# Attention outputs for two heads at a time, the own keys' products on 32-row tiles

## The chip, the cores and the metric

The kernel runs on one core of a Trainium2 chip. The metric is the device time of one execution in microseconds (us), the median of several runs. The whole model fragment is one program; the changed part is its attention stage.

## The reference, cut to what matters

Four layers are applied to a state of 64 sequences of 32 tokens and 512 features, each added to the state. The first three are a dense layer that is picked by sequence and two low-rank layers. The fourth is attention with a paged cache. Of it the change touches the line that starts `o =`:

```python
valid = jnp.concatenate([valid_c, jnp.ones((bsz, seqlen), dtype=bool)], axis=1)
k_all = jnp.concatenate([kc, k], axis=1)      # 512 cached keys, then the 32 own keys
v_all = jnp.concatenate([vc, v], axis=1)
k_all = jnp.repeat(k_all, rep, axis=2)        # 8 key heads, each for 4 query heads
v_all = jnp.repeat(v_all, rep, axis=2)
scores = jnp.einsum('bqhd,bkhd->bhqk', q, k_all) * SCALE
scores = jnp.where(valid[:, None, None, :], scores, -1e+30)
probs = jax.nn.softmax(scores, axis=-1)
o = jnp.einsum('bhqk,bkhd->bqhd', probs, v_all)
```

## The kernel before, in words

The program goes through the layers one after the other; attention takes from about 887 us to about 2106 us of the profiled execution.

**Units.** Attention works on units. A unit is one sequence and one key head: 4 query heads x 32 tokens are its 128 query rows, against 544 keys (512 cached and 32 own). There are 64 sequences x 8 key heads (HK) = 512 units. The main loop runs over pairs of sequences, that is 16 units (UNITS), numbered j = 0 to 15 in the pair; u is the unit's number in the whole run. I call the part of the loop body for one j a step, and count steps by j modulo 8.

**A step of TensorE (PE).** For each j it issues, in this order:
1. `scores` of unit u + 2: six matmuls of 128 x 272, three for each half of the keys, since both operands are split into a high and a low part (L102, L103, L104). They go to `ps_s`, half j % 2.
2. `outputs` of unit u - 4 (OG = 4): four fp32 matmuls of 128 x 128 against the cached values (L1672), and one against the own values (L1675). The trace shows every fp32 matmul as two weight loads (LDWEIGHTS) and two MATMUL records.
3. `transpose` of unit u: four 128 x 128 transposes of its probabilities into `ps_pt` (L1649). In steps 3 and 7 a transpose of the own keys' probabilities of the last four units follows (L1655), and in step 7 one of the sums of the probabilities (L1657).

**The own keys.** The own keys' probabilities of four units are put side by side (`p_own`, 4 x 32 columns), and transposed in one piece, so the 128 rows of `pto_sb` hold the 32 keys of unit 0, then those of unit 1, and so on. The own values `vo_sb` lie on the same 32 rows for each unit and are zero on the other 96, so before the change a product over all 128 rows gives the 32 keys' share. That transpose is written to a spare corner of `ps_s` (function `spare`), which is in the bank that the scores of the odd unit u + 2 also use. For that reason `transpose` waits ahead of L1655 until VectorE has read these scores:

```python
if j % OG == OG - 1:
    if not (last and j == UNITS - 1):
        pe.wait_ge(masked, u + 3)
    pe.wait_ge(gathered, u + 1)
    mm = pe.transpose(spare(1, P), p_own[:, g % 2, :, :].rearrange("p u k -> p (u k)"), ident[:, :])
```

`masked` counts the units whose scores VectorE has turned into masked, scaled scores with their maximum, so u + 3 means that unit u + 2 is done.

**VectorE (DVE)** in a step: in steps 0 and 4 the copy of the transposed own probabilities (`copy_own`, L1588), in step 0 also the reciprocal of the sums (L1595); then it waits for the scores of u + 2, gathers the own probabilities of u + 1 (L1580, waits for ScalarE's exponential of that unit), masks u + 2 (L1390), makes the low part of one piece of the next keys or queries (L1365; pieces stand in steps 0, 1, 2, 3, 4 and 7, the one in step 1 a short one, none in 5 and 6), copies the outputs of four units (`copy_o`, L1603, in steps 1 and 5), and in step 2 makes a mask (L1384).

**ScalarE (ACT)** in a step: the exponential of u + 2 (L1370), the high part of a piece (L1359), the copy of the transposed probabilities of u (L1548). **GpSimd (POOL)** issues the loads of queries, own keys and own values (L1484), the indirect loads of cached values (L1490) and the store of the outputs (L1496). SyncE (SP) issues the loads of key pages.

Semaphores set the order between the engines; each engine goes through its own list strictly in order. `pv_done` counts units whose outputs are finished, `o_ready` counts copies of outputs, `pt_ready` and `pto_ready` the copies of transposed probabilities.

Of the kernel before, what the change touches and what calls it, by code (L numbers as in the profile page):

```python
# [25 lines left out]
P = 128  # L26
NSEQ, SEQ, D = 64, 32, 512
# [6 lines left out]
DH, HQ, HK = 128, 32, 8  # L34
REP = HQ // HK
NPAGE, PSIZE, NPP = 64, 32, 16
NKEY = NPP * PSIZE
# [69 lines left out]
def later(t, n):  # L107

    return not isinstance(t, int) or t >= n
# [1133 lines left out]
UNITS = 2 * HK  # L1243
OG = 4
# [27 lines left out]
def attention(nc, m, place, both, pool_sems, k_pages, v_pages, table, lens, key_at, q_t, k_own, v_own, o_t, inv_t):  # L1272
# [37 lines left out]
    pv_done = m.sem("pv_done")  # L1310
# [10 lines left out]
    def group_before(i, j, n):  # L1321

        g = j // OG - n
        return (i, g) if g >= 0 else (i - 1, g + UNITS // OG)

    def spare(half, rows):

        return ps_s[0:rows, 1, half, D - P:D]
# [133 lines left out]
    def gpsimd(pool):  # L1462
# [29 lines left out]
                    bass.IndirectOffsetOnAxis(ap=rows_now[:, p, c:c + 1], axis=0)).then_inc(v_loaded[p], 16)  # L1492

        def store(s, p):
            pool.wait_ge(o_ready, (HK // OG) * (s + 1))
            pool.dma_start(o_t[bass.ds(s, 1)], o_sb[:, p, :, :].rearrange("p h q -> p (h q)"))\  # L1496
                .then_inc(o_stored[p], 16)
            pool.wait_ge(inv_ready, s + 1)
            pool.dma_start(inv_t[bass.ds(s, 1)].rearrange("s (h q) -> (s h) q", h=HK), inv_sb[:, p, :])\
                .then_inc(inv_stored[p], 16)  # L1500
# [67 lines left out]
    def vector(dve):  # L1568
# [25 lines left out]
                dve.wait_ge(inv_stored[p], 16 * i)  # L1594
            dve.reciprocal(inv_sb[:, p, :], spare(0, HK)).then_inc(inv_ready, 1)  # L1595

        def copy_o(i, g):

            p = g // 2
            dve.wait_ge(pv_done, UNITS * i + OG * (g + 1))  # L1600
            if later(i, 1):
                dve.wait_ge(o_stored[p], 16 * i)
            dve.tensor_copy(o_sb[:, p, (g % 2) * OG:(g % 2 + 1) * OG, :], ps_o[:, g % 2, :, :])\  # L1603
               .then_inc(o_ready, 1)

        dve.wait_ge(s_done, 2)
        gather(0, 0)
# [2 lines left out]
        def pair(i, last):  # L1610
            for j in range(UNITS):
                u, s, p = UNITS * i + j, 2 * i + j // HK, j // HK
                if j % OG == 0 and later(u, OG):
                    copy_own(*group_before(i, j, 1))
                    if j % HK == 0:
                        invert(*group_before(i, j, 1)[:1], (1 - p))
                if not (last and j >= UNITS - 2):
                    wait_for_scores(2 * i + (j + 2) // HK, u + 2, (j + 2) % UNITS)
                if not (last and j >= UNITS - 1):
                    gather(u + 1, (j + 1) % UNITS)  # L1620
                if not (last and j >= UNITS - 2):
                    mask_and_max(dve, u + 2, (j + 2) % UNITS)
                if not later(u, HK - 1):
                    for c in FIRST_LO[j]:
                        lo_part(dve, 1, 1, c)
                elif not (last and j >= HK - 1):
                    ahead = 2 if j % HK == HK - 1 else 1
                    for c in LO_AT[j % HK]:
                        lo_part(dve, s + ahead, (p + ahead) % 2, c)
                if j % OG == 1 and later(u, 2 * OG):  # L1630
                    copy_o(*group_before(i, j, 2))
                if j % HK == 2 and not (last and p):
                    make_mask(dve, s + 1, 1 - p)
            if last:
                copy_own(i, UNITS // OG - 1)
                invert(i, 1)
                copy_o(i, UNITS // OG - 2)
                copy_o(i, UNITS // OG - 1)

        in_pairs(dve, NSEQ // 2, pair)  # L1640

    def tensor(pe):
# [14 lines left out]
                mm = pe.transpose(spare(0, HK), total[:, p, :], ident[:, :])  # L1657
            mm.then_inc(t_done, 1)

        def outputs(i, u, j):  # L1660
            p, h, g = j // HK, j % HK, j // OG
            if h == 0:
                pe.wait_ge(v_loaded[p], 16 * (NPP // PPP) * (i + 1))
                pe.wait_ge(own_v_loaded[p], 16 * OG * (i + 1))
            if j % OG == 0 and later(u, 2 * OG):
                pe.wait_ge(o_ready, (UNITS // OG) * i + g - 1)
            pe.wait_ge(pt_ready, u + 1)
            if not later(u, 1):
                pe.wait_ge(both.out_ready, ALL_STEPS)
            out = ps_o[:, g % 2, j % OG, :]  # L1670
            for c in range(NKEY // P):
                pe.matmul(out, v_sb[p][:, c, h * DH:(h + 1) * DH], pt_sb[:, j % OG, c, :],  # L1672
                          start=(c == 0), stop=False)
            pe.wait_ge(pto_ready, UNITS // OG * i + g + 1)
            pe.matmul(out, vo_sb[p][:, g % 2, j % OG, :], pto_sb[:, g % 2, :],  # L1675
                      start=False, stop=True).then_inc(pv_done, 1)

        pe.wait_ge(both.normed_ready, ALL_STEPS)

        def pair(i, last):  # L1680
            for j in range(UNITS):
                u = UNITS * i + j
                if not (last and j >= UNITS - 2):
                    scores(pe, i + (j + 2) // UNITS, u + 2, (j + 2) % UNITS)
                if j >= OG:
                    outputs(i, u - OG, j - OG)
                elif later(u, OG):
                    outputs(i - 1, u - OG, UNITS - OG + j)
                transpose(u, j, last)
            if last:  # L1690
                for j in range(UNITS - OG, UNITS):
                    outputs(i, UNITS * i + j, j)

        in_pairs(pe, NSEQ // 2, pair)

# [303 lines left out]
```

## Time and profile before

| | |
|---|---|
| median of 3 runs | 2503.28 us (2501.54 to 2503.5) |
| the profiled execution, its own time | 2503.97 us |
| its span in the trace | 2502.3 us |
| PE busy / weight loads / DVE / ACT / POOL, share of the span | 96% / 88% / 71% / 64% / 24% |
| stretch of attention in the steady loop | 918.9 to 2100.6 us |

The span is the time from the first to the last instruction in the trace; the other 1.7 us of that execution lie around it. Busy shares are means over all stages; attention is nearly half of the time and is read by itself below.

### The profile page before, as it was taken

To read this page: it belongs to the slowest core of one execution; us is meant where nothing else is said; L and a number is where in the kernel's file an instruction comes from. 1 tells how busy PE (TensorE), PEld (TensorE's weight loads), DVE (VectorE), ACT (ScalarE), POOL (GpSimd) and SP (SyncE) were. 2 spreads that over 40 slices of the span, in tenths; PEclk is the share of its full clock that TensorE was granted. 3 is DMA by queue.
4 is the path that set the end of the run, shared out by engine and by line. 5 is a ranking of instruction groups with operands and counts; after the bars stand their busy time and mean duration, and the time that the engine had idled before them with its cause. 6 is when DMAs were issued, how large, how long until landed. Compare 5 with 4: busy or idle time off the path is not lost. (4 is left out here: it accounts for less than half of the span.)

```text
span 2502.3 us, 54645 instructions
## 1 busy us (share of the span) xinstructions
PE 2406.1 (96%) x16070; PEld 2192.6 (88%) x16071; DVE 1780.0 (71%) x3632; ACT 1603.3 (64%) x3311; POOL 599.2 (24%) x896
## 2 busy tenths in 40 slices
PE   6899899999999979999999999999999996799999
PEld 4688788888888879999999999999999996588887
DVE  5454329999898968878878878878878875544443
ACT  3233337777787778888888888888888884311111
POOL 1200040000000044444444444444444441000000
PEclk9899999999999979999999999999999998899999
DMA  6622333333334388888888888888888874766664
GB/s 221 185 81 64 117 122 90 101 102 97 100 114 124 94 289 300 289 288 303 291 289 300 289 290 301 293 288 302 291 287 294 300 255 156 281 210 221 208 209 145
DMA packets 373752, 536.83 MB, mean 215 GB/s; under 512 B 49314, under 2 KB 263010, under 8 KB 369826
## 3 DMA queue, kind: packets, MB, share of 16 engines
q1 hardware_dynamic: 301538, 311.62, 38.8%
q0 software_dynamic: 70016, 221.30, 25.8%
q10 hardware_dynamic: 2112, 2.89, 0.4%
q8 instruction: 38, 0.62, 0.1%
q14 instruction: 48, 0.39, 0.1%
HBM read 437.35 MB, written 98.30 MB: 214 GB/s over the span
## 5 line engine op out<-in xcount | busy, mean ns | idle before, releaser
L1672 PE MATMUL both_ps_o<-att_pt,att_v 128*128 128x128 f32 x4096 | 540.1, 275 | 0.0
L1370 ACT ACTIVATE att_prob<-att_prob,att_shift 128x544 f32<-128x544 f32 x512 | 384.4, 751 | 206.5 <-DVE att_shift L1390 197.0
L1672 PEld LDWEIGHTS both_ps_o<-att_pt,att_v 128*128 128x128 f32 x4096 | 504.8, 191 | 0.0
L1390 DVE CUSTOM_DVE_ANT_0 att_prob<-both_ps_s,att_mask 128x544 f32<-128x544 f32 x512 | 364.5, 712 | 0.0
L102 PE MATMUL both_ps_s<-att_k_hi,att_q_hi 128*128 128x272 f32 x1024 | 339.5, 332 | 4.6 <-DVE att_k_lo L1365 4.6
L1365 DVE TENSOR_TENSOR att_k_lo<-att_k_raw,att_k_hi 128x1024 fp32r<-128x1024 f32 (+1 forms) x320 | 338.5, 1058 | 1.9 <-ACT att_k_hi L1359 1.9
L1649 PE MATMUL both_ps_pt<-both_ident,att_prob 128*128 128x128 f32 x2048 | 309.4, 274 | 6.8 <-ACT att_prob L1370 5.2
L104 PE MATMUL both_ps_s<-att_k_hi,att_q_lo 128*128 128x272 f32 x1024 | 298.3, 291 | 0.0
L1548 ACT ACTIVATE att_pt<-both_ps_pt 128x512 f32<-128x512 f32 x512 | 294.6, 575 | 2.3 <-PE both_ps_s L1657 1.2
L103 PE MATMUL both_ps_s<-att_k_lo,att_q_hi 128*128 128x272 f32 x1024 | 295.4, 289 | 0.0
L1359 ACT ACTIVATE att_k_hi<-att_k_raw 128x1024 fp32r<-128x1024 f32 (+1 forms) x320 | 292.7, 915 | 0.0
L1484 POOL DMA_DIRECT2D att_vo<-v_own x256 | 139.9, 547 | 557.5 <-PE both_ps_o L1675 496.6
L1490 POOL DMA_INDIRECT att_v<-in_v_pages,att_rows_now x256 | 251.1, 981 | 86.0 <-issue 86.0
L1580 DVE TENSOR_REDUCE att_p_own<-att_prob 128x32 f32<-128x32 f32 x512 | 90.8, 177 | 237.0 <-PE both_ps_s L104 224.2
L1649 PEld LDWEIGHTS both_ps_pt<-both_ident,att_prob 128*128 128x128 f32 x2048 | 242.8, 142 | 7.5 <-ACT att_prob L1370 5.5
L1826 ACT ACTIVATE out_o_hi<-out_o 128x2048 fp32r<-128x2048 f32 x32 | 61.4, 1918 | 289.1 <-DVE out_o L1853 282.0
L102 PE MATMUL out_ps_y<-out_w_hi,out_o_hi 128*128 128x512 f32 x512 | 203.0, 397 | 36.2 <-DVE out_w_lo L1846 32.4
L103 PE MATMUL out_ps_y<-out_w_lo,out_o_hi 128*128 128x512 f32 x512 | 202.2, 395 | 0.0
L104 PE MATMUL out_ps_y<-out_w_hi,out_o_lo 128*128 128x512 f32 x512 | 202.0, 395 | 0.0
L102 PEld LDWEIGHTS both_ps_s<-att_k_hi,att_q_hi 128*128 128x128 f32 x1024 | 195.0, 190 | 6.8 <-DVE att_k_lo L1365 5.1
L1675 PE MATMUL both_ps_o<-att_pto,att_vo 128*128 128x128 f32 x1024 | 198.2, 275 | 0.0
L103 PEld LDWEIGHTS both_ps_s<-att_k_lo,att_q_hi 128*128 128x128 f32 x1024 | 196.2, 192 | 0.0
(209 smaller groups left out, 5025.7 us busy)
## 6 DMA issues: line engine op xcount, KB each, us to landing
att_k_raw<-in_k_pages SPq DMA_DIRECT2D x1024, 128.0 KB, 4.8
q_t<-qkv_out_t SPq DMA_DIRECT2D x128, 256.0 KB, 2.3
att_q_raw<-q_t POOLq DMA_DIRECT2D x64, 512.0 KB, 7.4
o_t<-att_o POOLq DMA_DIRECT2D x64, 512.0 KB, 6.9
out_o<-o_t SPq DMA_DIRECT2D x32, 1024.0 KB, 6.1
out_inv<-inv_t SPq DMA_DIRECT2D x32, 1024.0 KB, 6.6
both_w_stage<-in_w_qkv SPq DMA_DIRECT2D x12, 1024.0 KB, 5.2
l_w_stage<-in_w SPq DMA_DIRECT2D x8, 1024.0 KB, 7.1
```

What stands on the lines that cost most here:

```text
L102: pe.matmul(out, xh, wh, start=start, stop=False)
L103: pe.matmul(out, xh, wl, start=False, stop=False)
L104: return pe.matmul(out, xl, wh, start=False, stop=stop)
L1359: act.activation(hi, raw, ACT.Copy).then_inc(hi_done, 1)
L1365: dve.tensor_tensor(lo, raw, f32(hi), ALU.subtract).then_inc(lo_done, 1)
L1370: act.activation(prob[:, b, :], prob[:, b, :], ACT.Exp, bias=shift[:, b:b + 1], scale=-1.0, accum_out=total[:, j // HK, j % HK:j % HK + 1] ...
L1390: dve.tensor_tensor_reduce(out=prob[:, b, :].rearrange("p (a n) -> p a n", a=2), in0=ps_s[:, j % 2, :, 0:HALF], in1=mask[:, j // HK, :].re ...
L1490: pool.indirect_dma_start(v_sb[p][:, c, :], None, v_pages.rearrange("n k x -> (n k) x"), bass.IndirectOffsetOnAxis(ap=rows_now[:, p, c:c + ...
L1548: act.activation(pt_sb[:, j % OG, :, :], ps_pt[:, j % 2, :, :], ACT.Copy).then_inc(pt_ready, 1)
L1649: mm = pe.transpose(ps_pt[:, j % 2, c, :], prob[:, j % NB_P, c * P:(c + 1) * P], ident[:, :])
L1672: pe.matmul(out, v_sb[p][:, c, h * DH:(h + 1) * DH], pt_sb[:, j % OG, c, :], start=(c == 0), stop=False)
L1675: pe.matmul(out, vo_sb[p][:, g % 2, j % OG, :], pto_sb[:, g % 2, :], start=False, stop=True).then_inc(pv_done, 1)
```

## The change

The outputs are no longer made one unit a step. In every second step (j even) PE makes the outputs of two units, and in the others none. Each of the two units has a PSUM bank of its own (`ps_o[:, 0, 0, :]` and `ps_o[:, 1, 0, :]`). The eight products against cached values come first, then the two against own values; these now use the unit's own 32 rows of `vo_sb` and `pto_sb` alone, so that the two lie on different groups of 32 rows of the array. VectorE copies the two outputs together, 256 columns, at the end of the same step (before: 512 columns for four units, every fourth step). PE waits for that copy before the next two outputs. The store waits for four copies a sequence instead of two.

```diff
+    def units_before(i, j):
+
+        return (i, j - OG) if j >= OG else (i - 1, j - OG + UNITS)
...
-            pool.wait_ge(o_ready, (HK // OG) * (s + 1))
+            pool.wait_ge(o_ready, (HK // 2) * (s + 1))
...
-        def copy_o(i, g):
-
-            p = g // 2
-            dve.wait_ge(pv_done, UNITS * i + OG * (g + 1))
+        def copy_o(i, j):
+
+            p, h = j // HK, j % HK
+            dve.wait_ge(pv_done, UNITS * i + j + 2)
             if later(i, 1):
                 dve.wait_ge(o_stored[p], 16 * i)
-            dve.tensor_copy(o_sb[:, p, (g % 2) * OG:(g % 2 + 1) * OG, :], ps_o[:, g % 2, :, :])\
-               .then_inc(o_ready, 1)
+            dve.tensor_copy(o_sb[:, p, h:h + 2, :], ps_o[:, :, 0, :]).then_inc(o_ready, 1)
...
-                if j % OG == 1 and later(u, 2 * OG):
-                    copy_o(*group_before(i, j, 2))
+                if j % 2 == 0 and later(u, OG):
+                    copy_o(*units_before(i, j))
...
-        def outputs(i, u, j):
-            p, h, g = j // HK, j % HK, j // OG
-            if h == 0:
+        def outputs(i, j):
+
+            u, p, g = UNITS * i + j, j // HK, j // OG
+            if j % HK == 0:
                 pe.wait_ge(v_loaded[p], 16 * (NPP // PPP) * (i + 1))
                 pe.wait_ge(own_v_loaded[p], 16 * OG * (i + 1))
-            if j % OG == 0 and later(u, 2 * OG):
-                pe.wait_ge(o_ready, (UNITS // OG) * i + g - 1)
-            pe.wait_ge(pt_ready, u + 1)
+            if later(u, 2):
+                pe.wait_ge(o_ready, UNITS // 2 * i + j // 2)
             if not later(u, 1):
                 pe.wait_ge(both.out_ready, ALL_STEPS)
-            out = ps_o[:, g % 2, j % OG, :]
-            for c in range(NKEY // P):
-                pe.matmul(out, v_sb[p][:, c, h * DH:(h + 1) * DH], pt_sb[:, j % OG, c, :],
-                          start=(c == 0), stop=False)
+            for n in range(2):
+                h = (j + n) % HK
+                pe.wait_ge(pt_ready, u + n + 1)
+                for c in range(NKEY // P):
+                    pe.matmul(ps_o[:, n, 0, :], v_sb[p][:, c, h * DH:(h + 1) * DH], pt_sb[:, (j + n) % OG, c, :],
+                              start=(c == 0), stop=False)
             pe.wait_ge(pto_ready, UNITS // OG * i + g + 1)
-            pe.matmul(out, vo_sb[p][:, g % 2, j % OG, :], pto_sb[:, g % 2, :],
-                      start=False, stop=True).then_inc(pv_done, 1)
+            for n in range(2):
+                own = slice((j + n) % OG * SEQ, ((j + n) % OG + 1) * SEQ)
+                pe.matmul(ps_o[:, n, 0, :], vo_sb[p][own, g % 2, (j + n) % OG, :], pto_sb[own, g % 2, :],
+                          start=False, stop=True).then_inc(pv_done, 1)
...
-                if j >= OG:
-                    outputs(i, u - OG, j - OG)
-                elif later(u, OG):
-                    outputs(i - 1, u - OG, UNITS - OG + j)
+                if j % 2 == 0 and later(u, OG):
+                    outputs(*units_before(i, j))
                 transpose(u, j, last)
```

The order of instructions on PE, in a step 3 inside a sequence, with the step after it up to its first outputs. Names in brackets are the semaphores waited for; L1649, L1655, L1672 and L1675 of before are L1652, L1658, L1677 and L1682 after the change. Before:

```order
L104 MATMUL both_ps_s<-att_k_hi_4906,att_q_lo_4908 128x272
L1672 MATMUL both_ps_o<-att_pt,att_v_4910 128x128 [waits att_pt_ready]
L1672 MATMUL both_ps_o<-att_pt,att_v_4910 128x128 x3
L1675 MATMUL both_ps_o<-att_pto,att_vo_4911 128x128 [waits att_pto_ready]
L1649 MATMUL both_ps_pt<-both_ident,att_prob 128x128 [waits att_pt_ready,att_exp_done]
L1649 MATMUL both_ps_pt<-both_ident,att_prob 128x128 x3
L1655 MATMUL both_ps_s<-both_ident,att_p_own 128x128 [waits att_gathered,att_masked]
L102 MATMUL both_ps_s<-att_k_hi_4906,att_q_hi_4907 128x272 [waits att_masked]
```

After:

```order
L104 MATMUL both_ps_s<-att_k_hi_4906,att_q_lo_4908 128x272
L1652 MATMUL both_ps_pt<-both_ident,att_prob 128x128 [waits att_pt_ready,att_exp_done]
L1652 MATMUL both_ps_pt<-both_ident,att_prob 128x128 x3
L1658 MATMUL both_ps_s<-both_ident,att_p_own 128x128 [waits att_gathered,att_masked]
L102 MATMUL both_ps_s<-att_k_hi_4906,att_q_hi_4907 128x272 [waits att_masked]
```

Between the last scores matmul (L104) and the transpose of the own probabilities, which waits for `masked`, the five output matmuls are gone; they stand in the step before, with those of another unit.

On VectorE, at the end of a step 2 and the start of step 3 (L1365, L1384, L1580 and L1390 of before are L1369, L1388, L1584 and L1394 after). Before:

```order
L1365 TENSOR_TENSOR att_k_lo_4909<-att_k_raw_4904,att_k_hi_4906 128x4x8x32 [waits att_hi_done]
L1384 ISA
L1384 TENSOR_SCALAR att_mask<-att_key_at,att_lens_f 128x512
L1573 REGISTER_ALU
L1580 TENSOR_REDUCE att_p_own<-att_prob 128x32 [waits att_exp_done,att_t_done,att_s_done]
```

After:

```order
L1369 TENSOR_TENSOR att_k_lo_4903<-att_k_raw_4898,att_k_hi_4900 128x4x8x32 [waits att_hi_done]
L1607 COPY att_o<-both_ps_o 128x256 [waits pool_o_stored0,att_pv_done]
L1388 ISA
L1388 TENSOR_SCALAR att_mask<-att_key_at,att_lens_f 128x512
L1577 REGISTER_ALU
L1584 TENSOR_REDUCE att_p_own<-att_prob 128x32 [waits att_exp_done,att_t_done,att_s_done]
```

A copy of two units' outputs now stands in step 2, as in steps 0, 4 and 6, ahead of the gather and the masking of the next step.

## Rows read from the trace of the kernel before

**Rows 1.** The page's first part: busy time, share of the span, instructions.

```profile
PE 2406.1 (96%) x16070; PEld 2192.6 (88%) x16071; DVE 1780.0 (71%) x3632; ACT 1603.3 (64%) x3311; POOL 599.2 (24%) x896
```

**Rows 2.** Windows: busy us and instructions of each engine, clock, DMA share, GB/s.

```profile
1501.25:1520.02 18.77, 18.77 (x166) 18.75 (x164) 15.22 (x37) 15.62 (x31) 8.49 (x14) 1.00 0.85 293
918.90:2100.60 1181.70, 1181.70 (x10260) 1180.30 (x10259) 953.44 (x2256) 978.19 (x1881) 529.32 (x804) 1.00 0.86 287
```

**Rows 3.** Line L1657, once a sequence: duration in ns, first and last start.

```profile
L1657 PE MATMUL both_ps_s<-both_ident,att_total x64: 272/273/273, 919.0 to 2100.7; 128*8 128x128 f32 x64
```

**Rows 4.** Waits, 918.9 to 2100.6 us: us, times, longest. PE has none.

```profile
DVE att_p_own L1580 <- PE both_ps_s L104: 219.5, 285, 1.5
ACT att_prob L1370 <- DVE att_shift L1390: 192.2, 285, 1.3
POOL att_vo L1484 <- PE both_ps_o L1675: 496.6, 61, 14.5
```

**Rows 5.** Timeline of a step 3: start, duration (us), engine, line.

```profile
1508.88 0.29 PE L104 MATMUL both_ps_s<-att_k_hi,att_q_lo 128*128 128x272 f32 x1
1508.89 0.98 PEld L1672 LDWEIGHTS both_ps_o<-att_pt,att_v 128*128 128x128 f32 x8
...
1509.33 0.18 DVE L1580 TENSOR_REDUCE att_p_own<-att_prob 128x32 f32<-128x32 f32 x1
1509.43 0.71 DVE L1390 CUSTOM_DVE_ANT_0 att_prob<-both_ps_s,att_mask 128x544 f32<-128x544 f32 x1
...
1509.79 0.30 PEld L1675 LDWEIGHTS both_ps_o<-att_pto,att_vo 128*128 128x128 f32 x2
...
1510.01 0.47 PEld L1649 LDWEIGHTS both_ps_pt<-both_ident,att_prob 128*128 128x128 f32 x4
1510.07 0.08 DVE L1390 DVE_READ_ACCUMULATOR2_ANT att_shift<- 128x1 f32 x1
...
1510.19 0.75 ACT L1370 ACTIVATE att_prob<-att_prob,att_shift 128x544 f32<-128x544 f32 x1
1510.45 0.14 PEld L1655 LDWEIGHTS both_ps_s<-both_ident,att_p_own 128*128 128x128 f32 x1
...
1510.56 0.19 PEld L102 LDWEIGHTS both_ps_s<-att_k_hi,att_q_hi 128*128 128x128 f32 x1
...
1510.84 0.19 ACT L1370 ACTIVATION_READ_ACCUMULATOR att_prob<-att_prob,att_shift 128x1 f32 x1
...
1511.29 0.29 PE L104 MATMUL both_ps_s<-att_k_hi,att_q_lo 128*128 128x272 f32 x1
```

**Rows 6.** Timeline of the first step 3, where no outputs exist yet.

```profile
904.65 0.43 PE L104 MATMUL both_ps_s<-att_k_hi,att_q_lo 128*128 128x272 f32 x1
...
906.68 0.08 DVE L1390 DVE_READ_ACCUMULATOR2_ANT att_shift<- 128x1 f32 x1
...
906.81 0.18 PEld L1655 LDWEIGHTS both_ps_s<-both_ident,att_p_own 128*128 128x128 f32 x1 [1.26 <-DVE att_shift L1390]
```

**Rows 7.** Timeline around L1657, whose weights are 8 columns instead of 128.

```profile
1501.11 0.09 PEld L1657 LDWEIGHTS both_ps_s<-both_ident,att_total 128*8 128x8 f32 x1
1501.22 0.27 PE L1657 MATMUL both_ps_s<-both_ident,att_total 128*8 128x128 f32 x1
1501.22 0.19 PEld L102 LDWEIGHTS both_ps_s<-att_k_hi,att_q_hi 128*128 128x128 f32 x1
```

**Rows 8.** Groups by form, 1000 to 1800 us: busy us, mean ns.

```profile
L1675 PE MATMUL both_ps_o<-att_pto,att_vo 128*128 128x128 f32 x682 | 131.9, 275 | 0.0
L1603 DVE COPY att_o<-both_ps_o 128x512 f32<-128x512 f32 x85 | 58.2, 685 | 0.0
L1588 DVE COPY att_pto<-both_ps_s 128x128 f32<-128x128 f32 x85 | 24.1, 283 | 0.0
L1365 DVE TENSOR_TENSOR att_k_lo<-att_k_raw,att_k_hi 128x1024 fp32r<-128x1024 f32 x170 | 206.9, 1217 | 0.0
L1384 DVE TENSOR_SCALAR att_mask<-att_key_at,att_lens_f 128x512 f32<-128x512 f32 x43 | 20.6, 480 | 0.0
```

**Rows 9.** Windows at the start of attention; columns as in rows 2.

```profile
903.00:909.00 6.00, 5.14 (x24) 4.66 (x23) 5.22 (x15) 5.67 (x12) 5.30 (x8) 0.50 0.96 302
916.00:920.00 4.00, 4.00 (x37) 3.98 (x36) 2.57 (x8) 3.81 (x7) 0.00 (x0) 1.00 1.04 392
```

More of the change, by code:

```diff
@@ L1636, in pair @@
                 invert(i, 1)
-                copy_o(i, UNITS // OG - 2)
-                copy_o(i, UNITS // OG - 1)
+                for j in range(UNITS - OG, UNITS, 2):
+                    copy_o(i, j)
         in_pairs(dve, NSEQ // 2, pair)
@@ L1684, in pair @@
                     scores(pe, i + (j + 2) // UNITS, u + 2, (j + 2) % UNITS)
-                if j >= OG:
-                    outputs(i, u - OG, j - OG)
-                elif later(u, OG):
-                    outputs(i - 1, u - OG, UNITS - OG + j)
+                if j % 2 == 0 and later(u, OG):
+                    outputs(*units_before(i, j))
                 transpose(u, j, last)
             if last:
-                for j in range(UNITS - OG, UNITS):
-                    outputs(i, UNITS * i + j, j)
+                for j in range(UNITS - OG, UNITS, 2):
+                    outputs(i, j)
         in_pairs(pe, NSEQ // 2, pair)
```

## The prediction

> **What bounds the kernel now.** I read the page first: TensorE (PE) is busy for 96% of the span, everything else for 71% or less [rows 1]. A mean over stages proves little, so I read the attention loop by itself. One sequence takes 18.76 us: line L1657 runs once a sequence, 63 intervals between 919.0 and 2100.7 [rows 3]. In such a stretch PE is busy for all 18.77 us and its weight loads for 18.75, at full clock, while VectorE (DVE) works 15.22 and ScalarE (ACT) 15.62 [rows 2]. The waits agree: in the whole loop PE waits for nobody, while DVE waits 219.5 us for scores and ACT 192.2 us for DVE [rows 4]. So the loop goes at PE's pace; time taken from PE is gained and time in which PE stands is lost, one for one.
>
> The timeline of one step gives PE's parts, from one weight load to the next group's [rows 5]: the eight records against cached values 1508.89 to 1509.79, 0.90 us or 0.112 us a slot; the two of the own product 0.22; four transposes 1510.01 to 1510.45, 0.44; the own probabilities' transpose 0.11; the six score matmuls 1510.56 to 1511.29, 0.73. Without the extra transpose a step is 0.90 + 0.22 + 0.44 + 0.73 = 2.29 us.
>
> **What the change takes away.** The number of matmuls stays the same. A pair of units' own products takes 4 slots, 0.45 us. On 32 rows each still loads 128 columns and streams 128 columns, so alone it has no reason to be shorter; a gain comes only if the two units' products run beside each other on different rows. No row of the trace shows two row groups at work, so I bound it. No overlap: 4 slots, gain 0. Full overlap: 2 slots, 0.22 us a pair, 256 pairs, 57 us. Since each product is two records that must follow each other on the same rows, the second record of the first can overlap the first record of the second: 3 slots, 0.11 us a pair, 28 us. I take 3, in the middle between two ends for which no row speaks.
>
> In the Trainium skill, "TensorE: Matmul & The Clock Gate", Part 3, matmuls on different row groups run concurrently, and their weight loads overlap matmuls in flight; by it the pair would come near 2 slots and the gain near 57 us. No run here shows it yet.
>
> Changing between 128-row and 32-row tiles may cost something. The nearest row is L1657, whose weights are 8 columns wide instead of 128: its load starts at 1501.11, its matmul 0.11 us later, and the next full-width load at that same 1501.22 [rows 7]. Narrowing and widening cost nothing there, but in columns, not rows. Taken as it stands that row gives 0. The upper bound is that PE runs empty at each change: a record lasts 0.275 us [rows 8] against a slot of 0.11, so 0.165 us of tail, and 0.11 us more if the next weights can't load under it. Twice a pair, 256 pairs, is 84 to 141 us. I take 0 by the nearest row and keep the rest as a rival.
>
> The Trainium skill, "TensorEngine Tiling (Array Packing)", Key Properties, states that changing the tiling mode drains TensorE. By that rule the sum grows by those 84 to 141 us. The trace does not agree for the column case [rows 7].
>
> **What it moves, and the wait that this uncovers.** In steps 3 and 7, ahead of L1655, PE waits for `masked` of the unit whose scores it issued at the start of that same step. Let T be the start of the last score matmul, 1508.88. DVE gathers at T + 0.45 (1509.33), masks from 1509.43, and its accumulator read ends at 1510.15, T + 1.27 [rows 5]. PE gets to L1655's load at 1510.45, T + 1.57, because 0.90 + 0.22 of outputs and 0.44 of transposes stand between. So the wait has 0.30 us to spare. After the change steps 3 and 7 are odd steps: no outputs. PE gets there at T + 0.44 and stands until T + 1.27, plus some 0.05 for the release. In the first step 3, which has no outputs before the change either, exactly this wait is seen: the read ends at 906.76, the load starts at 906.81 after 1.26 us idle [rows 6]. Price: 1.27 + 0.05 - 0.44 = 0.88 us, in 128 groups less the first (already without outputs) and the last (doesn't wait), 126 x 0.88 = **111 us**. Behind L1655 on PE stand the next scores, for which DVE waits, so nothing makes it good.
>
> **Is DVE itself late there?** An odd step without L1655 is now 0.44 + 0.73 = 1.17 us, an even one 1.80 + 0.33 + 0.44 + 0.73 = 3.30. Step 2's gather needs the exponential of unit u + 1, which ACT makes from step 1's mask: that ends at T1 + 1.27, and ACT is done 0.88 us after such an end (1510.15 to 1511.03 [rows 5]). So the gather starts at T1 + 2.15, which is T2 + 0.98 instead of T2 + 0.45. Then DVE needs 0.82 for gather and mask, 1.22 for the low part, 0.42 for the copy and 0.48 for the mask of the next sequence [rows 8]: done at T2 + 3.92. T3 + 0.45 is T2 + 3.75. So in step 3 DVE is 0.17 us late, and PE's wait grows by as much once a sequence: 63 x 0.17 = 11 us. With 4 slots for the own products it is 0.06 (4 us), with 2 slots 0.28 (18 us). Step 7 follows a step with neither a low part nor a mask, and DVE is on time.
>
> **Edits at no cost.** A copy of 256 columns I put at 0.42 us: 0.283 for 128 and 0.685 for 512 [rows 8] give 0.134 for each further 128. Four a sequence instead of two are 1.67 against 1.37, so 0.30 us more for DVE, of 3.5 us that it is idle in 18.77 [rows 2]; outside step 2 idle time covers it. It costs PE only if it delays the next two outputs. These wait for the copy. In step 0 DVE is busy with copy, reciprocal, gather, mask, low part and ends the copy about T0 + 3.7; the next outputs come at T0 + 3.30 + 1.17 = T0 + 4.5: 0.8 us to spare. In steps 2, 4 and 6 there is more. GpSimd's loads of own values start when a sequence's outputs are done; it waits 496.6 us for that [rows 4], 8 us a sequence, and the outputs finish in step 2 instead of 3: hidden. The store of the outputs waits for a copy that now comes three steps earlier. The wait of PE for `pto_ready` moves behind eight more records, so it only gets easier.
>
> **The sum**, against the profiled execution's own 2503.97 us, which is 0.7 above the median of 2503.28: the wait +111, DVE's lateness +11, the own products -28, together +94: 2598 for such an execution, **2597 us** for the median. With 4 slots +111 + 4, 2618; with 2 slots +111 + 18 - 57, 2575.
>
> **Rivals.**
> - *The row tiles don't overlap* (the change doesn't do what it says): 2618. That a record's load already takes the whole slot of its matmul (weight loads 18.75 of 18.77 us [rows 2]) speaks for it: if loads go one by one, nothing is gained. It is one end of my forecast.
> - *The tile change empties PE.* 84 to 141 us on 2618, or on 2597 if the products overlap as well: 2681 to 2759. Against it: rows 7. For it: these are rows of the array, through which data flow, not columns.
> - *The clock falls.* At the start of attention, with PE standing now and again (busy 5.14 of 6.00 us), the granted clock was 0.50; with PE without gaps it was 1.00 [rows 9]. New gaps of about 0.9 to 1.2 us stand twice in some 20. Were a tenth of the loop's 1182 us of PE work done at 1.2 GHz instead of 2.4, that would add 118 us: about 2715. Against it: some 9 us of unbroken work between gaps.
> - *DVE becomes the bound.* If small gaps between its instructions grow with the new order by 0.5 us a sequence and reach PE, 32 us more: about 2629.
> - *Faster, on the other side:* the wait costs nothing since `masked` comes early. It decides from the point where stall and gain of a group of two pairs are equal: the release must come less than 0.44 + 0.22 = 0.66 us (3 slots) or 0.44 + 0.44 = 0.88 us (2 slots) after T, instead of 1.32. If it came within 0.44, the time would be 2503 - 28 = 2475, or 2446. Against it: the mask alone takes 0.71 us, and it can't start before the scores are done.
>
> **How the numbers follow.** My forecast, the wait of 0.88 us or a little more with own products in 2 to 4 slots, has a chance of 0.72: 2575 to 2618, with the small terms 2560 to 2635. The emptied PE gets 0.14, the clock 0.03, DVE as the bound 0.06, the faster case 0.05. The point is the likeliest's middle, 2597. The range reaches down to 2558 and up to 2670, which leaves out most of the emptied PE, the clock and the faster case, together 0.2. A measurement of this kernel tells about 0.2% (5 us) from no change. Faster by more: 0.05; within: 0.02; slower: 0.93.
>
> **What would show it.** Right: the waits list PE at the own probabilities' transpose (now L1658), released by DVE's shift, about 126 times, 0.9 us each, 110 to 130 us in all; a sequence takes about 20.3 us; the second of the own products' records start less than 0.11 us apart where row groups change. Wrong: no such wait, or a gap of 0.15 us or more between the last cached product, the own ones and the transposes (the tile change costs), or a clock under 1.00 in the loop. The forecast of the main term fails if DVE's reading of the scores ends much sooner than 1.27 us after T, or if PE comes later to L1658 than T + 0.44.

## The result and the profile after

The changed kernel takes 2635.4 us (median of 4 runs, 2633.8 to 2636.9), the kernel before 2503.4 (4 runs): a ratio of 1.0526, 95% interval 1.0508 to 1.0545, so 132 us slower. The profiled execution took 2635.22 us with a span of 2633.7.

The page's first part of the changed kernel, against [rows 1]:

```profile
PE 2471.8 (94%) x16070; PEld 2159.7 (82%) x16071; DVE 1804.0 (68%) x3760; ACT 1603.1 (61%) x3311; POOL 657.0 (25%) x896
```

TensorE (PE) issues the same 16070 matmuls, but its share fell. VectorE (DVE) has 128 more instructions, the additional copies. The windows, columns as in [rows 2], show the whole loop and one sequence:

```profile
920.40:2230.80 1310.40, 1249.18 (x10258) 1149.51 (x10259) 977.53 (x2382) 978.85 (x1881) 586.91 (x804) 1.00 0.77 258
1503.80:1524.60 20.80, 19.84 (x164) 18.36 (x165) 15.74 (x39) 15.74 (x31) 9.51 (x13) 1.00 0.81 273
```

The line that runs once a sequence and the two products, by tile (duration min/median/max in ns, first and last start), against [rows 3]:

```profile
L1660 PE MATMUL both_ps_s<-both_ident,att_total x64: 272/273/273, 920.5 to 2230.9; 128*8 128x128 f32 x64
L1682 PE MATMUL both_ps_o<-att_pto,att_vo x1024: 269/321/373, 911.0 to 2236.1; 32*128 32x128 f32 x171
L1607 DVE COPY att_o<-both_ps_o x256: 404/423/426, 911.5 to 2236.5; 128x256 f32<-128x256 f32 x128
```

A sequence takes (2230.9 - 920.5) / 63 = 20.80 us instead of 18.76. That is 2.04 us more, and 64 times 2.04 is 131 us: the whole loss is in this loop. Its granted clock is still 1.00, that is 2.4 GHz. The loop has 1310.4 us, and PE is busy for 1249.2 of them where it had been busy without a gap; but the busy time itself also grew by 67 us with as many matmuls, so the listed gaps needn't be all of it. Busy time rests on modelled ends of matmuls; below I go by the starts of weight loads.

The waits from 920 to 2200 us, nearly the whole loop (us, times, longest), against [rows 4] where PE had none:

```profile
POOL att_vo L1488 <- PE both_ps_o L1682: 560.1, 60, 15.3
ACT att_prob L1374 <- DVE att_shift L1394: 249.2, 369, 1.0
DVE att_p_own L1584 <- PE both_ps_s L104: 146.9, 184, 0.9
DVE att_p_own L1584 <- ACT att_prob L1374: 102.0, 123, 1.0
PEld both_ps_s L1658 <- DVE att_shift L1394: 88.5, 123, 0.7
DVE att_o L1607 <- PE both_ps_o L1682: 61.1, 122, 0.8
PE both_ps_s L1658 <- DVE att_shift L1394: 59.4, 123, 0.5
PEld both_ps_s L102 <- issue: 9.2, 29, 0.3
```

The forecast wait is there: at the transpose of the own probabilities (now L1658), released by DVE's shift, 123 times in 61.5 sequences, that is in every group. PE's weight loads stand 0.72 us each time. DVE also waits 61.1 us for the products at its new copies; no wait of PE for these copies is listed, so that costs nothing. The last line is new: 29 times 0.3 us of "issue" ahead of scores, which nobody releases.

The timeline of an even step and of the following step 3 of the changed kernel, against [rows 5] (start, duration, engine, line; in brackets the idle time before and its releaser):

```profile
1504.64 1.88 PEld L1677 LDWEIGHTS both_ps_o<-att_pt,att_v 128*128 128x128 f32 x16
1506.64 0.30 PEld L1682 LDWEIGHTS both_ps_o<-att_pto,att_vo 32*128 32x128 f32 x4
1506.65 0.49 PE L1682 MATMUL both_ps_o<-att_pto,att_vo 32*128 32x128 f32 x4
1507.06 0.42 PEld L1652 LDWEIGHTS both_ps_pt<-both_ident,att_prob 128*128 128x128 f32 x4
1507.45 0.19 PEld L102 LDWEIGHTS both_ps_s<-att_k_hi,att_q_hi 128*128 128x128 f32 x1
...
1512.68 0.48 DVE L1388 TENSOR_SCALAR att_mask<-att_key_at,att_lens_f 128x512 f32<-128x512 f32 x1
1512.93 0.29 PE L104 MATMUL both_ps_s<-att_k_hi,att_q_lo 128*128 128x272 f32 x1
1512.94 0.48 PEld L1652 LDWEIGHTS both_ps_pt<-both_ident,att_prob 128*128 128x128 f32 x4
1513.26 0.19 DVE L1584 TENSOR_REDUCE att_p_own<-att_prob 128x32 f32<-128x32 f32 x1
1513.36 0.72 DVE L1394 CUSTOM_DVE_ANT_0 att_prob<-both_ps_s,att_mask 128x544 f32<-128x544 f32 x1
1514.00 0.08 DVE L1394 DVE_READ_ACCUMULATOR2_ANT att_shift<- 128x1 f32 x1
1514.14 0.14 PEld L1658 LDWEIGHTS both_ps_s<-both_ident,att_p_own 128*128 128x128 f32 x1 [0.72 <-DVE att_shift L1394]
1514.22 0.19 PEld L102 LDWEIGHTS both_ps_s<-att_k_hi,att_q_hi 128*128 128x128 f32 x1
```

Two things are to be seen. In the even step, 16 slots of cached values should take 1.81 us by [rows 5], and the first load on 32 rows should come at 1506.45; it comes at 1506.64, 0.19 us late. The four products on 32 rows then last 0.42 us until the transposes' load at 1507.06, though they overlap: a narrower window of the same timeline has the second pair of their loads only 0.11 us behind the first.

```profile
1506.75 0.19 PEld L1682 LDWEIGHTS both_ps_o<-att_pto,att_vo 32*128 32x128 f32 x2
```

In the step without outputs the own transpose stands from about 1513.38 until 1514.14, 0.06 us after DVE's read of its accumulator ends (1514.08).

To account for a sequence I averaged, over some 60 of them, the time from the first weight load of each group of matmuls to that of the next. V: cached values, W: own products, T: transposes up to the next group, P: own probabilities' transpose, Q: transpose of the sums, S: scores.

```
per pair of units (us)      V      W      T       per sequence: T+P step 3   T+P step 7   Q      all
before                    1.808  0.444  0.439                   0.548        0.548        0.109  18.78
after                     1.998  0.420  0.388                   1.274        1.254        0.255  20.84
```

So of about 2.06 us a sequence: the change of row tile costs 0.19 us ahead of the own products, leaves these at 0.42 instead of the 0.22 that two slots take, and gives 0.05 back in the transposes: 0.115 a pair net or 0.46 a sequence (30 us in all). The wait is 0.726 + 0.706 = 1.43 (92 us). Q's stretch is 0.15 longer, which is the "issue" of the table above (9 us).

### The profile page after: what moved, and what is told of

The parts are those of the page before. It is cut to its first block and busy times, and to the rows that moved or that the text cites. A ratio compares the mean times of both kernels' runs of the same rounds, so it can differ in the third digit from the quotient of the medians.

```text
span 2633.7 us, 55206 instructions
## 1 busy us (share of the span) xinstructions
PE 2471.8 (94%) x16070; PEld 2159.7 (82%) x16071; DVE 1804.0 (68%) x3760; ACT 1603.1 (61%) x3311; POOL 657.0 (25%) x896
## 5 line engine op out<-in xcount | busy, mean ns | idle before, releaser
L1677 PE MATMUL both_ps_o<-att_pt,att_v 128*128 128x128 f32 x4096 | 499.5, 275 | 0.6 <-DVE att_o L1607 0.6
L1677 PEld LDWEIGHTS both_ps_o<-att_pt,att_v 128*128 128x128 f32 x4096 | 481.9, 192 | 0.8 <-DVE att_o L1607 0.7
L1394 DVE CUSTOM_DVE_ANT_0 att_prob<-both_ps_s,att_mask 128x544 f32<-128x544 f32 x512 | 364.6, 712 | 0.0
L1369 DVE TENSOR_TENSOR att_k_lo<-att_k_raw,att_k_hi 128x1024 fp32r<-128x1024 f32 (+1 forms) x320 | 338.8, 1059 | 4.3 <-ACT att_k_hi L1363 1.9
L1652 PE MATMUL both_ps_pt<-both_ident,att_prob 128*128 128x128 f32 x2048 | 322.8, 280 | 6.6 <-ACT att_prob L1374 5.0
L1494 POOL DMA_INDIRECT att_v<-in_v_pages,att_rows_now x256 | 306.0, 1195 | 81.2 <-issue 81.2
L104 PE MATMUL both_ps_s<-att_k_hi,att_q_lo 128*128 128x272 f32 x1024 | 297.4, 290 | 0.0
L1584 DVE TENSOR_REDUCE att_p_own<-att_prob 128x32 f32<-128x32 f32 x512 | 90.1, 176 | 275.1 <-PE both_ps_s L104 155.2
L1652 PEld LDWEIGHTS both_ps_pt<-both_ident,att_prob 128*128 128x128 f32 x2048 | 229.8, 141 | 38.1 <-ACT att_prob L1374 5.3
L104 PE MATMUL out_ps_y<-out_w_hi,out_o_lo 128*128 128x512 f32 x512 | 201.6, 394 | 0.0
L104 PEld LDWEIGHTS both_ps_s<-att_k_hi,att_q_lo 128*128 128x128 f32 x1024 | 194.3, 190 | 0.0
```

What stands on the lines that cost most here:

```text
L104: return pe.matmul(out, xl, wh, start=False, stop=stop)
L1369: dve.tensor_tensor(lo, raw, f32(hi), ALU.subtract).then_inc(lo_done, 1)
L1394: dve.tensor_tensor_reduce(out=prob[:, b, :].rearrange("p (a n) -> p a n", a=2), in0=ps_s[:, j % 2, :, 0:HALF], in1=mask[:, j // HK, :].re ...
L1494: pool.indirect_dma_start(v_sb[p][:, c, :], None, v_pages.rearrange("n k x -> (n k) x"), bass.IndirectOffsetOnAxis(ap=rows_now[:, p, c:c + ...
L1652: mm = pe.transpose(ps_pt[:, j % 2, c, :], prob[:, j % NB_P, c * P:(c + 1) * P], ident[:, :])
L1677: pe.matmul(ps_o[:, n, 0, :], v_sb[p][:, c, h * DH:(h + 1) * DH], pt_sb[:, (j + n) % OG, c, :], start=(c == 0), stop=False)
```

## Experiments

Two causes are to be told apart, and each has to be priced without the other. Theory: the wait for `masked` costs some 95 us, the tile change some 30 net of the overlap. Rivals: it is mainly the tile change (PE's busy time grew by 67 us); DVE or the copies set the pace; the new order costs something of its own. Each comparison below is with the kernel before on the same chip: the time, then the ratio with its 95% interval. Averages by group are made as above.

**The tiles without the wait's cause, and the wait without the tiles.** `e1_full_rows` keeps the new order and takes the own products on all 128 rows:

```diff
-                own = slice((j + n) % OG * SEQ, ((j + n) % OG + 1) * SEQ)
+                own = slice(0, P)
```

> The changed kernel with the own keys' products over all 128 rows again (zeros on the other 96), all else as changed: two units in every second step, two banks, the copy by pairs. By my theory the narrow products cost time, about 0.19 us on entering them and 0.20 on leaving, less 0.22 for the overlap and 0.05 in the transposes: 0.12 us a pair, 256 pairs, 30 us. So 2605 (2600 to 2610), and PE's step parts are 1.81 (cached), 0.45 (own), 0.44 (transposes) as before. Rival: the extra 0.19 us ahead of the own products is the wait for pto_ready or for a bank, not the tile change, and the overlap is a plain gain. Then the time is 2635 or more, up to 2690.

2601.6 us, ratio 1.0399 [1.0382, 1.0417], as the theory expected. V, W and T are back at 1.80, 0.446 and 0.439, and the wait is the same:

```profile
PEld both_ps_s L1658 <- DVE att_shift L1394: 89.8, 125, 0.7
PE both_ps_s L1658 <- DVE att_shift L1394: 60.2, 125, 0.5
PEld both_ps_s L102 <- issue: 9.2, 29, 0.3
```

The order alone costs 99 us, the tiles 1.27% of 2503, 32 us. `e6_transpose_first` uses the kernel before, its tiles and its outputs in each step, and only lets the transposes go ahead of the outputs, so that the own transpose loses its cover in another way:

```diff
                     scores(pe, i + (j + 2) // UNITS, u + 2, (j + 2) % UNITS)
+                transpose(u, j, last)
                 if j >= OG:
...
-                transpose(u, j, last)
```

> The kernel before with one edit: in each step PE transposes unit u before it makes the outputs of unit u - 4, so in steps 3 and 7 no outputs stand between the scores and the wait for masked, with one unit's outputs a step and 128-row tiles throughout. By my theory PE stands there as in the changed kernel, 0.75 us less 0.03 in 126 groups, 91 us: 2594 (2585 to 2610). Rival: the wait of the changed kernel comes from the two-unit order (DVE is held up by copies that wait for PE), then it is 2503 to 2515 here.

2593.7 us, 1.0366 [1.0349, 1.0383].

```profile
PEld both_ps_s L1655 <- DVE att_shift L1390: 93.0, 125, 0.8
PE both_ps_s L1655 <- DVE att_shift L1390: 63.5, 125, 0.6
```

No pairing, no copy by pairs, no row tile, and the same wait at the same price, 91 us in all. Here outputs stand between the stall and the next scores, Q's stretch stays at 0.111 us, and the "issue" line is missing. The 9.2 us of that line are about the 8 us that separate it from e1.

**The same outputs in odd steps.** `e3_odd_steps` covers the own transpose again by moving outputs and copies one step on; `e4_odd_full` is the same with full rows.

```diff
-                if j % 2 == 0 and later(u, OG):
-                    outputs(*units_before(i, j))
+                if j % 2 == 1 and later(u, OG + 1):
+                    outputs(*units_before(i, j - 1))
```

> The changed kernel with the two units' outputs, and their copy, in the odd steps instead of the even ones, so that they stand between the scores and the wait for masked in steps 3 and 7 again; own products on 32 rows as changed. By my theory the wait vanishes (0.75 us twice a sequence) and with it the gap at the loop's end: only the tile change is left over before, 2503 + 30, that is 2533 (2528 to 2550). Rival: what costs is that outputs come in lumps of two units, for which DVE's and ACT's chains are late somewhere; then it stays at 2600 or more, whatever step they stand in.

> As the one with the outputs in odd steps, and the own products over all 128 rows: neither of my two costs is left. 2503 (2498 to 2515). Rival, lumps of two units cost by themselves: 2570 or more.

2567.5 us, 1.0263 [1.0246, 1.0280], and 2543.7, 1.0165 [1.0148, 1.0182]: 34 and 41 us above what was expected. The wait for `masked` is gone, and another has come, for the reciprocal of the sums (of e3, then of e4):

```profile
PEld both_ps_s L102 <- DVE att_inv L1599: 23.7, 60, 0.4
```

```profile
PEld both_ps_s L102 <- DVE att_inv L1599: 26.6, 60, 0.5
```

Steps 0 and 4 now have no outputs, and the scores behind their transposes overwrite the spare columns that DVE must first read (own probabilities and sums). T before these scores is 0.87 us in step 0 and 0.53 in step 4. So the even placement has the mirror image of the same fault. The expectation was wrong in that I had looked at one bank hand-over only. The difference of the two ratios is 0.98%, 25 us: the tile change again, 7 less than above, because without it PE comes earlier and waits longer (T 0.92 instead of 0.87 us in step 0, 0.60 instead of 0.53 in step 4).

**The own transpose one step later.** `e5_defer` takes the two transposes out of steps 3 and 7 and puts them behind the scores of the next step, with a semaphore of their own; DVE copies them after its mask. `e9_defer_full` is the same with full rows.

```diff
-            if j % OG == OG - 1:
-
-                if not (last and j == UNITS - 1):
-                    pe.wait_ge(masked, u + 3)
...
+                if j % OG == 0 and later(u, OG):
+                    transpose_own(*group_before(i, j, 1))
                 if j % 2 == 0 and later(u, OG):
```

> The changed kernel (two units in even steps, 32-row own products) with one thing moved: the transposes of the own probabilities and of the sums leave steps 3 and 7 and stand in the next step, behind its scores, which go to the other half of ps_s; they signal on a semaphore of their own, and VectorE copies and inverts after it has masked that step's scores. PE then comes to the wait for masked at T + 1.28 us, where T + 1.2 is needed. By my theory the 0.75 us wait and the gap at the loop's end are gone, and the inverse, whose lateness stopped PE in the odd-step kernels, has two units' outputs to hide under. What is left is the tile change: 2503 + 34 = 2537 (2530 to 2548). Rival: lumps of two units make something else late, as in the odd steps; 2560 or more.

> The same with own products over all 128 rows, so with neither cost: 2503 (2498 to 2512). Rival as above: 2530 or more.

2551.6 us, 1.0194 [1.0175, 1.0212], and 2528.0, 1.0097 [1.0079, 1.0115]: 15 and 25 us above what was expected. The wait is no longer listed, and 83 us of the changed kernel's loss have gone with it (1.0526 less 1.0194), but 24 us stay with full rows, where 0 was expected. The averages of e9 place them: in step 4 the scores take 0.87 instead of 0.74 us and the own transpose 0.32 instead of 0.11; in step 0 the scores take 0.79. Of e9, a wait and a step 4:

```profile
PEld both_ps_o L1680 <- issue: 7.4, 30, 0.3
```

```profile
1524.52 0.08 DVE L1394 DVE_READ_ACCUMULATOR2_ANT att_shift<- 128x1 f32 x1
1524.65 0.14 PEld L1661 LDWEIGHTS both_ps_s<-both_ident,att_p_own 128*128 128x128 f32 x1
```

The list names only what stands between the own transpose and the outputs of step 4. The late scores are the old wait in small: in three of four groups the own transpose's load starts 0.05 us after DVE's accumulator read ends, as it does in the changed kernel. So PE still comes just too early to the wait for `masked`. The two kernels differ by 0.97%, 24 us and not 32, since PE comes later to this wait in e5, where the scores of step 4 take 0.75 us.

`e13_cover_more`, made from e9, puts the ordinary transposes ahead of the own one in steps 0 and 4, to cover it:

```diff
                 if j % OG == 0 and later(u, OG):
+                    transpose(u, j, last)
                     transpose_own(*group_before(i, j, 1))
...
-                transpose(u, j, last)
+                if not (j % OG == 0 and later(u, OG)):
+                    transpose(u, j, last)
```

> The deferred kernel with 128-row own products (2528, where I expected 2503), with unit u's transposes moved ahead of the deferred transposes in steps 0 and 4. What that kernel still loses, 0.42 us a sequence, I read as PE coming to the wait for masked just in time: it stands shortly, its queue runs empty, and the waits and register instructions ahead of the next outputs show. With 0.44 us of transposes more as cover that must go: 2505 (2500 to 2510). Rival, two units' outputs in one step cost these 25 us by themselves, or the added semaphore does: 2520 to 2530.

2518.5 us, 1.0060 [1.0046, 1.0073]. It gained 9 of the 24 us and lies 8 above the expected range and just under the rival's. DVE's read now ends some 0.36 us or more ahead of the own transpose's load. In all other steps each group is within 0.02 us of the kernel before (V and W taken together); step 4 keeps 0.11 us ahead of its transposes and 0.13 between the own transpose and the outputs, and has 0.05 back within the transposes. From the timeline of a step 4:

```profile
1517.64 0.58 ACT L1552 ACTIVATE att_pt<-both_ps_pt 128x512 f32<-128x512 f32 x1
1518.34 0.42 PEld L1652 LDWEIGHTS both_ps_pt<-both_ident,att_prob 128*128 128x128 f32 x4
1518.73 0.14 PEld L1661 LDWEIGHTS both_ps_s<-both_ident,att_p_own 128*128 128x128 f32 x1
1519.02 1.64 PEld L1680 LDWEIGHTS both_ps_o<-att_pt,att_v 128*128 128x128 f32 x14 [0.15 <-issue]
```

The late transposes are one more hand-over. PE's program lets them start once ScalarE has copied the transposes of step 2 (`pt_ready`); their first load comes 0.11 us after the end of that copy in every one of some 60 sequences, where in all other steps the copy ends 0.5 us or more before. The outputs' load comes 0.29 us after the last instead of 0.11, and nothing that the profile shows releases it. These outputs, a sequence's first, have four waits ahead of them in PE's program, where others have two; that these take the time is a guess. No order tried here beats the kernel before.

**The price of a tile change by itself.** `e7_64_rows` uses 64 rows, both units of a pair on the same ones, so that the two can't run beside each other. `e8_four_changes` puts each unit's own product right behind its cached ones, so that a pair goes into 32 rows and back twice.

```diff
-                own = slice((j + n) % OG * SEQ, ((j + n) % OG + 1) * SEQ)
+                own = slice(j % OG // 2 * 2 * SEQ, (j % OG // 2 + 1) * 2 * SEQ)
```

```diff
-            pe.wait_ge(pto_ready, UNITS // OG * i + g + 1)
-            for n in range(2):
+                pe.wait_ge(pto_ready, UNITS // OG * i + g + 1)
                 own = slice((j + n) % OG * SEQ, ((j + n) % OG + 1) * SEQ)
```

> The changed kernel, but the two own products of a pair both use the 64 rows of their two units (the other unit's rows of vo are zero), so the tile changes as often but the two can't run beside each other. If entering and leaving a narrower tile cost 0.19 and 0.20 us whatever its rows, and the overlap of 32-row tiles is worth 0.22, a pair takes 0.22 us more than in the changed kernel: 2635 + 57 = 2692 (2680 to 2705). Rival, the two 32-row products do not overlap and the change costs little: 2635 within 10.

> The changed kernel with each unit's own product right behind its cached ones, so that a pair changes the tile four times instead of two and nothing overlaps. By my theory a pair takes 0.19 + 0.20 us more for the two further changes and 0.22 less overlap, with 0.05 back where a load can start early: 0.56 us, 256 pairs, 143 us: 2778 (2755 to 2795). Rival, the 0.2 us come once a pair from something else than the change of tile: 2635 to 2695.

2689.9 us, 1.0748 [1.0729, 1.0767], and 2788.6, 1.1139 [1.1119, 1.1159]. The own products by tile, of e7 and then of e8:

```profile
L1682 PE MATMUL both_ps_o<-att_pto,att_vo x1024: 272/272/373, 910.3 to 2290.4; 64*128 64x128 f32 x171
```

```profile
L1681 PE MATMUL both_ps_o<-att_pto,att_vo x1024: 269/322/373, 909.1 to 2390.0; 32*128 32x128 f32 x171
```

Against e1, which has the same order on full rows, e7 is slower by 3.49% (87 us; 256 round trips, 0.34 us each) and e8 by 7.40% (185 us; 512 round trips, 0.36 each). The changed kernel itself is slower than e1 by 0.124 us a pair, which is 0.34 less the 0.22 that two overlapping slots save. By groups e7 has V +0.20, W +0.19, T -0.05 against e1. Its four records of the own products take 0.638 us a pair up to the transposes, those of the changed kernel 0.420: the 0.22 between them is the overlap. So 64 rows cost what 32 do, the price is per change, and three kernels agree on it.

**How much slack the wait has.** An extra reduction of DVE on its scratch, between gather and mask of steps 3 and 7, delays `masked`. `e10_after_one` adds it to the changed kernel, `e11_before_one` and `e12_before_two` add one and two to the kernel before.

```diff
                     gather(u + 1, (j + 1) % UNITS)
+                    for n in range(1 if j % OG == OG - 1 else 0):
+                        dve.tensor_reduce(extra[:, j // OG, n, :], prob[:, (j + 1) % NB_P, 0:384].rearrange("p (a b) -> p a b", b=12), AX.X, ALU.max)
```

> The changed kernel with one extra reduction of 128 x 384 on VectorE (its result is not used), in steps 3 and 7 between the gather and the mask of the unit for which PE waits. I put it at 0.42 us from the durations of DVE's other reads of SBUF. By my theory PE's wait is set by DVE's chain from the last score matmul to the mask, so it grows by all of it, twice a sequence: 126 x 0.42 = 53 us, 2635 to 2688 (2680 to 2700). Rival, PE stands for something else that ends at about the same time: 2635 to 2645.

> The same extra reduction in the kernel before, where the outputs stand ahead of the wait. In a step 3 masked comes 0.30 us early, 0.25 with the release, in a step 7, where DVE is not late, some 0.37. So of 0.42 us only 0.17 and 0.05 come through: 14 us a run, 2517 (2505 to 2525), a quarter of what it costs in the changed kernel.

> Two such reductions in the kernel before, 0.84 us: the slack is used up, 0.59 and 0.47 come through, 67 us: 2570 (2555 to 2585). Rival to the slack of 0.25 to 0.37 us: the work costs in proportion, so twice what one costs.

2694.3 us, 1.0758 [1.0740, 1.0777]; 2523.5, 1.0074 [1.0055, 1.0092]; 2582.6, 1.0314 [1.0297, 1.0331]. The waits of e10, e11 and e12:

```profile
PEld both_ps_s L1661 <- DVE att_shift L1395: 139.0, 118, 1.2
```

```profile
PEld both_ps_s L102 <- issue: 9.2, 29, 0.3
PEld both_ps_s L1658 <- DVE att_shift L1391: 5.5, 30, 0.2
```

```profile
PEld both_ps_s L1658 <- DVE att_shift L1391: 69.0, 125, 0.6
```

In the changed kernel the full extra is paid at once: T grows from 1.194 to 1.653 us, by 0.459. The kernel before takes the first one for 0.154 in step 3 and 0.097 in step 7 and the second for 0.459 in each. So its slack, from the release to PE's arrival, was 0.459 - 0.154 = 0.305 us in step 3 and 0.36 in step 7. The 0.305 is a mean of two kinds of sequence, which alternate: 0.245 in one and 0.36 in the other, where DVE isn't late. The change took away 1.13 us of outputs as cover; 1.13 - 0.36 is 0.77, and 0.755 was measured. The "issue" line appears as soon as PE stands in step 7 at all, however short: in e11 it is 9.2 us of the 18 lost.

## Why the prediction was right, and where not

It was right in sign, and in the mechanism and the place of its main term, and 38 us too low. The time lies at the upper edge of what the likeliest forecast allowed (2635), and inside the range, which reaches on to 2670. One of its own signs of being wrong came true: the gap of 0.15 us or more around the own products, 0.19 and 0.20. That the sum came as near as it did is luck in part: its three misses of +58, -30 and +9 us, told below, partly cancel.

- *What bounds the kernel*: right. PE sets the pace before and, with its gaps, after; the order of DVE's and ScalarE's work does not.
- *The wait* (+111): right in place, and present in practically every group, but too large in size. Predicted 0.88 us in each of 126; measured 0.755 longer before the own transpose, 0.73 and 0.71 once the shorter P behind it is counted, 92 us. The mis-sized part is the release at T + 1.27. It was read from [rows 5], a step 3 in which DVE had just ended the next mask and started its gather late. That is the case in the step 3 of every second sequence only; in the other three of four groups DVE's read ended at T + 1.15 before the change too, as in this step 3 of the kernel before, one sequence later:

```profile
1527.66 0.29 PE L104 MATMUL both_ps_s<-att_k_hi,att_q_lo 128*128 128x272 f32 x1
1528.73 0.08 DVE L1390 DVE_READ_ACCUMULATOR2_ANT att_shift<- 128x1 f32 x1
1529.23 0.14 PEld L1655 LDWEIGHTS both_ps_s<-both_ident,att_p_own 128*128 128x128 f32 x1
```

After the change it is T + 1.15 in all groups (1513.26 for the gather and 1514.08 for the end, after 1512.93). With it the prediction's own sum gives 1.15 + 0.05 - 0.44 = 0.76 us. Its slack of 0.30 us leaves out the 0.05 of the release; that e11 gives 0.305 is chance, a mean of 0.245 and 0.36.

- *DVE late in step 3* (+11): wrong, it is 0. Steps 3 and 7 have the same T, 1.194 and 1.195. The reasoning took an even step for 3.30 us; with the tile change it is 1.998 + 0.420 + 0.388 + 0.738 = 3.54, 0.24 more; and DVE's chain begins 0.12 earlier, with a mask that ends at T + 1.15. Together that is 0.36, more than the 0.17. e1, with an even step of 3.42, also shows 1.194 in both.
- *Own products, 3 slots of 4* (-28): too cautious as to the overlap. Four loads start in two pairs 0.11 us apart, between 1506.64 and 1507.06; two slots, the bound of -57. The same four records on shared rows take 0.22 us more (e7). By the Trainium skill, "TensorE: Matmul & The Clock Gate", Part 3, matmuls on different row groups run concurrently: the trace agrees, 0.42 us a pair being 0.22 and the way out of the tile.
- *The tile change at 0* (bounds 0 and 84 to 141): this is the step that failed. It costs 0.34 us a round trip, 0.19 to 0.20 before, as much behind and 0.05 given back, 87 us for 256 pairs (e7), about where the bounds began. With the overlap's -57 it makes the net +30 to 32, where I had -28 in the sum: 58 us of error, of which wait and lateness gave back 30. The choice was led by [rows 7], a tile that is narrower in columns. The prediction itself noted that columns and rows differ, and still let the nearest row decide. By the Trainium skill, "TensorEngine Tiling (Array Packing)", Key Properties, a change of the tiling mode drains TensorE: the traces agree for 128 rows to 32 or 64 and back, with a price of 0.34 us, though none shows the draining itself.
- *Clock, DVE as the bound, copies, GpSimd, stores*: right. The clock is 1.00 in the loop, the copy takes 423 ns (0.42 predicted), and 560 us of GpSimd's waiting show how far it is from mattering.
- *Not foreseen*: the 9 us of "issue" at the loop's end. With it the sum is 92 + 30 + 9 = 131, of 132.

Both causes are shown apart (e1 and e6 for the wait, e7 and e8 for the tile). Not tried: 32-row products in the order of the kernel before, and DVE's mask ahead of its gather. Of the 15 us that remain in e13, the part ahead of step 4's transposes is a wait for ScalarE; the part ahead of its outputs is placed but not explained.

## What to carry to other kernels

When work is moved between steps, look at every semaphore wait that stands behind its old place and write down how many tenths of a microsecond it has to spare; here one had 0.25 to 0.36 us and lost 1.1 of cover twice a sequence, and moving the work one step further only took the cover from another. Read such a slack in several places of the loop: one timeline showed the latest of four cases. Where a change gives up the full row tile, count its entries and exits: here a pair must save more than 0.34 us, and two overlapping slots save 0.22. And price an operation that no row shows between its bounds, not by the row that merely looks alike.

## What the runs showed of the hardware

- Going from products on 128 rows to 32 or 64 and back costs 0.19 to 0.20 us each way, less 0.05 in the loads behind: 0.34 us in the changed kernel and e7, 0.36 in e8. A change from 128 to 8 columns cost nothing [rows 7].
- Products on different groups of 32 rows overlap fully: without the way out of the tile, four records take 0.22 us, where on the same 64 rows they take 0.44 (0.420 against 0.638 with it), and their loads start in pairs.
- Where PE stands in step 7, however short (0.10 us in e11), the loop's end behind it costs 0.3 us of "issue", in every second sequence, as one pass of the loop makes two. It is absent where PE doesn't stand directly ahead of it (before, e3, e4), and where outputs lie between (e6). Why isn't shown.
- A DVE record of 0.543 us (the extra reduction, `att_extra`, median in e10) delays what follows by 0.459: consecutive records overlap by 0.08 to 0.09, as the gather and the mask do (1513.26 + 0.19 against 1513.36).
- PE's load starts 0.05 us after the end of DVE's accumulator read that releases it, and 0.11 us after the end of ScalarE's copy (e13).
